# A recurrent block on one core: the third q/k unit and one constant row moved ahead of the second half's transposes, with other PSUM banks around them

## The chip, the core and the metric

The kernel runs on one NeuronCore of a Trainium2 chip. Its engines work side by side and meet only at semaphores: TensorE (PE; its weight loads are listed as PEld), VectorE (DVE), ScalarE (ACT), GpSimd (POOL), and SyncE (SP), which here only issues DMAs. Products land in PSUM, eight banks of 128 x 512 f32. The metric is the device time of one execution, in microseconds (us), as the median of three runs.

## What is computed

The input is (4, 1024, 128) in f32. Two layers, each `x + s(xn) * silu(f(xn))`, with xn the row-normalised x:

```python
# layer 0: attention in x with a bilinear score, times silu of a gated ternary MLP (512 hidden)
x = x + s * g
xn = _layernorm(x, axis=-1)
# layer 1, s: recurrence over 1024 steps, 8 heads of 64
q, k, v = xn @ Wq + bq, xn @ Wk + bk, xn @ Wv + bv
attn = softmax_over_heads(einsum('bhd,bhd->bh', q_t, k_t) * scale)
state = decay * state + (1 - decay) * attn[..., None] * v_t
out = layernorm((q * states + sigmoid(q * aug)) @ Wo + bo)
# layer 1, f: attention with 16 heads of 8 over 1024 tokens, plus top-2 of 8 experts
x = x + out * silu(attn_out + moe_out)
```

## The kernel before, in words

The four batch rows run one after the other (`for b in range(B)`), and each engine has its own program with an order written out by hand. Every value that needs more precision than one pass gives is carried as a high and a low part, so one product is three matmuls (`split3`). A "half" is 512 of the 1024 tokens.

Within a batch, layer 0 comes first, and ends with `residual(c)`, `block_stats(c)` and `block_normalise(c)` on DVE for each half c. POOL takes the inverse root of the variance between the last two (L866). PE then transposes the normalised half (`transposes`, L1110) into `T_BANKS[c]`, ACT copies the high part out (`split_head`, `xt_hi`, L944), DVE the rest (`split_rest`, `xt_lo`, L459).

Layer 1 is prepared by the part that the change touches, the bridge:

- `mq_units(c)` on PE: k and q of the 16-head attention for one half, four matmuls that need only the high part and two that need the low part, into `MQ_BANKS`. ACT adds the bias (`mq_head`, into `spl`, L999), DVE takes the low part (`mq_rest`, L548) and the largest absolute value (`mq_maximum`, L556).
- `qk_unit(u)` on PE: unit u of q and k of the recurrence, six matmuls of 512 columns into the two banks `QK_BANKS[u]`. ACT copies q (`q_unit`, into `qz`, L994), DVE multiplies by k (`product`, L541). Units 0 to 4 are in the bridge, 5 to 7 beside the attention. Units 0 to 3 read the first half only, so unit 2 needs neither the second half's transposes nor its split.
- `values_unit(0)` on PE and `values_in(0)` on DVE (L569, L574): the values of the first three token tiles.
- a bound of the scores: `bnd_in` after the four maxima, a product with ones on PE, a few small operations on DVE (from L611), `bnd_ok`.
- `stack(i)` on PE and `stacked(i)` on ACT (L1008, L1010), i = 0 to 3: the rows of the first group of four heads, with q and k for both halves. `stack(i)` needs `mq_rest(i)`.
- constant rows: ACT fills `k_st[:, g4, :]` for the groups 1 to 3 (three copies of 128 x 1024, L1027), POOL fills those of q after `bnd_ok` (L873).
- SP copies q and k of the groups 1 to 3 from `spl` to `k_st` and `q_st` in 72 small DMAs (L351). It starts when the three constant rows are filled and `mq_head(3)` is done.

The attention follows: 64 steps (`m_scores`, `m_values`), each with four score matmuls, four value matmuls and two exponentials on ACT (L1046), and a list `SIDE` of other pieces between them. Step 0 waits for `stacked(1)` and for `product(3)`, its order also puts it behind `stack(3)`, and it waits for a flag that DVE reads after `product(4)`. Step 16, the first of the second group of heads, waits until that group's DMAs have landed; these are among the first 64 of the 72.

PE's order in the bridge is: `mq_units(0)`, `g_transposes(1)`, `qk_unit(0)`, `qk_unit(1)`, `transposes(xnv, 6, 1)`, `values_unit(0)`, `mq_units(1)`, `qk_unit(2)`, `stack(0)`, the bound's product, `qk_unit(3)`, `stack(1)`, `stack(2)`, `qk_unit(4)`, `stack(3)`, step 0.

Of the kernel before, what the change touches and what calls it, by code (L numbers as in the profile page):

```python
# [14 lines left out]
ACT = mybir.ActivationFunctionType  # L15
# [6 lines left out]
B, S, D = 4, 1024, 128  # L22
NT = S // P
CH = 512
# [5 lines left out]
HM, HDM = 16, 8  # L30
# [17 lines left out]
H_BANKS = ((0, 1, 2, 3), (4, 5, 6, 7))  # L48
W3_BANKS, GT_BANKS = (0, 4), (1, 7)
PV_BANKS = (4, 5, 4, 5, 4, 5, 2, 3)  # L50
T_BANKS = (5, 6)
QK_BANKS = ((2, 3), (4, 5), (2, 3), (4, 5), (0, 1), (6, 7), (6, 7))
MQ_BANKS = (0, 1)
STK_BANKS = (6, 7, 6, 6)
NAT_LAST_BANK = 0
HEAD_ROWS = (slice(64, 80), slice(96, 112))

SIDE = {0: ("qk", 5), 1: ("qk", 6), 2: ("mv", 1), 3: ("q", 7), 4: ("mv", 2), 5: ("k", 7), 6: ("hs", 0), 7: ("hs", 1),
# [60 lines left out]
def build_program(nc, x, fw, lw, aw, wo, cst, cols, rows, bexp, out):  # L119
    with ExitStack() as ctx:  # L120
# [141 lines left out]
        def col(name, k=0):  # L262
            return cols_sb[:, COL[name] + k:COL[name] + k + 1]

        def up(signal, ins, n=1):

            signal.given += n
            return ins.then_inc(signal.sem, n)
# [96 lines left out]
        def _(v):  # L365
# [71 lines left out]
            for b in range(B):  # L437
# [19 lines left out]
                def split_rest(lo, hi, bank, c, sig_mm, n_mm, sig_hi, sig_lo):  # L457
                    v.wait_ge(sig_hi.sem, sig_hi.at(b, n_mm))
                    up(sig_lo, v.tensor_tensor(lo[:, c * CH:(c + 1) * CH], ps[:, bank, :],  # L459
                                               hi[:, c * CH:(c + 1) * CH].bitcast(F32), ALU.subtract))  # L460
# [75 lines left out]
                def product(u, bank):  # L536

                    c, m = u // KM, u % KM
                    v.wait_ge(qk_mm.sem, qk_mm.at(b, 2 * u + 2))
                    v.wait_ge(q_copy.sem, q_copy.at(b, u + 1))  # L540
                    up(prod_ok, v.scalar_tensor_tensor(prods[u], ps[:, bank, :], col("bk", m),  # L541
                                                       qz[:, m, c * CH:(c + 1) * CH], ALU.add, ALU.mult))

                def mq_rest(i):

                    c, j = i // 2, 1 - i % 2
                    v.wait_ge(mq_hi.sem, mq_hi.at(b, i + 1))
                    up(mq_lo, v.scalar_tensor_tensor(spl[:, 2 * j + 1, c * CH:(c + 1) * CH], ps[:, MQ_BANKS[i % 2], :],  # L548
                                                     col(("mbq", "mbk")[j]), spl[:, 2 * j, c * CH:(c + 1) * CH].bitcast(F32),
                                                     ALU.add, ALU.subtract))  # L550

                def mq_maximum(i):

                    c, j = i // 2, 1 - i % 2
                    v.wait_ge(mq_hi.sem, mq_hi.at(b, i + 1))
                    step(v.tensor_reduce(qk_max[:, 2 * j + c:2 * j + c + 1], spl[:, 2 * j, c * CH:(c + 1) * CH].bitcast(F32),  # L556
                                         AX.X, ALU.max, apply_absolute_value=True))
# [5 lines left out]
                def values_in(i):  # L563

                    tl = slice(3 * i, min(3 * i + 3, NT))
                    n_ = tl.stop - tl.start
                    v.wait_ge(mv_mm.sem, mv_mm.at(b, i + 1))
                    src = ps[:, SIDE_BANK, 0:n_ * (D + E)].rearrange("p (t n) -> p t n", n=D + E)
                    step(v.tensor_tensor(  # L569
                        vaug4[:, tl, :, 0:HDM], src[:, :, 0:D].rearrange("p t (h n) -> p t h n", n=HDM),  # L570
                        rows_sb[:, 3 * D:4 * D].rearrange("p (h n) -> p h n", n=HDM).unsqueeze(1)
                        .broadcast_to([P, n_, HM, HDM]), ALU.add))
                    own()
                    up(mv_ok, v.tensor_tensor(glog3[:, tl, :], src[:, :, D:D + E],  # L574
                                              rows_sb[:, 4 * D:4 * D + E].unsqueeze(1).broadcast_to([P, n_, E]), ALU.add))
# [15 lines left out]
                mq_rest(1)  # L591
                product(0, QK_BANKS[0][1])
                product(1, QK_BANKS[1][1])
                mq_maximum(0)
                mq_maximum(1)
                split_rest(xt_lo, xt_hi, T_BANKS[1], 1, xT_mm, 2, x_hi, x_lo)
                values_in(0)
                mq_maximum(2)
                mq_maximum(3)
                own()  # L600
# [3 lines left out]
                own()  # L604
                up(bnd_in, v.tensor_scalar(sm[:, 7, 0:HM], cst_sb[:, CBM:CBM + HM], qk_max[:, 6:7], None, ALU.mult))
                mq_rest(2)
                product(2, QK_BANKS[2][1])

                v.wait_ge(bnd_mm.sem, bnd_mm.at(b, 1))
                bound = ps[:, SIDE_BANK, 0:HM]  # L610
                step(v.tensor_reduce(flags[:, 1:2], bound, AX.X, ALU.min))  # L611
                own()
                step(v.tensor_scalar(flags[:, 2:3], flags[:, 1:2], -SAFE * HDM ** 0.5, None, ALU.is_ge))
# [298 lines left out]
        def _(a):  # L912
# [28 lines left out]
            for b in range(B):  # L941
                def split_head(hi, bank, c, sig_mm, n_mm, sig_hi):
                    a.wait_ge(sig_mm.sem, sig_mm.at(b, n_mm))
                    up(sig_hi, a.activation(hi[:, c * CH:(c + 1) * CH], ps[:, bank, :], ACT.Copy))  # L944
# [43 lines left out]
                def q_unit(u, bank):  # L988
                    c, m = u // KM, u % KM
                    if u == 0:  # L990
                        a.wait_ge(fin_ok.sem, fin_ok.at(b, 0))
                        a.wait_ge(stored.sem, stored.at(b, 0))
                    a.wait_ge(qk_mm.sem, qk_mm.at(b, 2 * u + 1))
                    up(q_copy, a.activation(qz[:, m, c * CH:(c + 1) * CH], ps[:, bank, :], ACT.Identity, bias=col("bq", m)))  # L994

                def mq_head(i):
                    c, j = i // 2, 1 - i % 2
                    a.wait_ge(mq_mm.sem, mq_mm.at(b, i + 1))
                    up(mq_hi, a.activation(spl[:, 2 * j, c * CH:(c + 1) * CH], ps[:, MQ_BANKS[i % 2], :], ACT.Identity,  # L999
                                           bias=col(("mbq", "mbk")[j])))  # L1000

                def stacked(i):
# [19 lines left out]
                mq_head(1)  # L1022
                q_unit(0, QK_BANKS[0][0])
                q_unit(1, QK_BANKS[1][0])
                for g4 in range(1, NG):
                    a.wait_ge(w3_mm.sem, w3_mm.at(b, 2))
                    up(kfill_ok, a.activation(k_st[:, g4, :], col("row24").broadcast_to([P, S]), ACT.Copy))  # L1027
                split_head(xt_hi, T_BANKS[1], 1, xT_mm, 2, x_hi)
                mq_head(2)
                mq_head(3)  # L1030
                q_unit(2, QK_BANKS[2][0])
                stacked(0)
                a.activation(mrow2[:, 0:1], ones[:, 0:1], ACT.Exp)
                q_unit(3, QK_BANKS[3][0])
                stacked(1)
                stacked(2)
                q_unit(4, QK_BANKS[4][0])
                stacked(3)

                for k_ in range(CYCLES):  # L1040
# [47 lines left out]
        def _(t_):  # L1088
# [9 lines left out]
            def with_high(out_, l_hi, l_lo, r_hi_):  # L1098

                mm(out_, l_hi, r_hi_, True, False)  # L1100
                mm(out_, l_lo, r_hi_, False, False)
# [38 lines left out]
            for b in range(B):  # L1140
# [6 lines left out]
                def lwp(at, n=P):  # L1147
                    return lw_hi[:, at:at + n], lw_lo[:, at:at + n]
# [158 lines left out]
                def mq_units(c):  # L1307

                    t_.wait_ge(x_hi.sem, x_hi.at(b, 1 + c))
                    for i, j in enumerate((1, 0)):  # L1310
                        with_high(ps[:, MQ_BANKS[i], :], *lwp(LM + j * D), xT(c)[0])
                    t_.wait_ge(x_lo.sem, x_lo.at(b, 1 + c))
                    for i, j in enumerate((1, 0)):
                        up(mq_mm, mm(ps[:, MQ_BANKS[i], :], lwp(LM + j * D)[0], xT(c)[1], False, True))

                def qk_unit(u):

# [12 lines left out]
                def values_unit(i):  # L1330

                    for t in range(3 * i, min(3 * i + 3, NT)):
                        at = (t % 3) * (D + E)
                        ins = split3(ps[:, SIDE_BANK, at:at + D + E], *tok(t), *lwp(LM + 2 * D, D + E))
                    up(mv_mm, ins)

                t_.wait_ge(lw_ok, 1)
# [2 lines left out]
                t_.wait_ge(pv_norm.sem, pv_norm.at(b, NT))  # L1340
                qk_unit(0)
                qk_unit(1)
                t_.wait_ge(ln_ok.sem, ln_ok.at(b, 2))
                transposes(xnv, T_BANKS[1], 1)
                values_unit(0)
                t_.wait_ge(mq_lo.sem, mq_lo.at(b, 2))
                mq_units(1)
                t_.wait_ge(prod_ok.sem, prod_ok.at(b, 1))
                qk_unit(2)
                stack(0)  # L1350
                t_.wait_ge(bnd_in.sem, bnd_in.at(b, 1))
                t_.wait_ge(mv_ok.sem, mv_ok.at(b, 1))
                up(bnd_mm, mm(ps[:, SIDE_BANK, 0:HM], ones, sm[:, 7, 0:HM], True, True))
                t_.wait_ge(prod_ok.sem, prod_ok.at(b, 2))
                qk_unit(3)
                t_.wait_ge(bnd_ok.sem, bnd_ok.at(b, 1))
                stack(1)
                t_.wait_ge(stk_ok.sem, stk_ok.at(b, 1))
                stack(2)
                t_.wait_ge(mq_lo.sem, mq_lo.at(b, 4))  # L1360
                qk_unit(4)
                t_.wait_ge(stk_ok.sem, stk_ok.at(b, 3))
                stack(3)

# [270 lines left out]
```

## Time and profile before

| what | us |
|---|---|
| median of three runs | 1064.15 (1063.66 to 1066.93) |
| the profiled execution | 1064.29 |
| its span, first to last instruction | 1062.5 |
| PE busy | 980.8 (92%) |
| ACT busy | 757.9 (71%) |
| DVE busy | 568.7 (54%) |
| POOL busy | 203.9 (19%) |

The profiled execution's own time is 1.8 us more than its span. The chain that ended last lies 72% on PE, 9% on DVE and 6% on ACT, so PE's queue sets most of the time, but the share is a mean over stages: in the bridge the chain passes from engine to engine. A batch takes some 255 us, and its bridge some 20.

### The profile page before, as it was taken

The page shows a single profiled execution, that of the slowest core. Times are in us where ns is not written, and L with a number is a line of the kernel's source. Part 1 is how long each engine was busy: PE and PEld are TensorE (multiplying, and loading weights), DVE is VectorE, ACT ScalarE, POOL GpSimd, SP SyncE. Part 2 cuts the span into 40 slices and gives each one's busy share as a digit, 9 for nine tenths or more (in the row PEclk, how much of TensorE's full clock was granted, in tenths as well). Part 3 has the DMA queues.
Part 4 walks back from the last instruction along what each step waited for, and adds up shares of the span by engine and source line. Part 5 has one row for each costly group of instructions (what it writes and reads, how often), then busy time and mean ns, then how long its engine had stood idle before and what let it go on. Part 6 is the DMA issues. An engine that isn't in the chain of part 4 may idle for free.

```text
span 1062.5 us, 16258 instructions
## 1 busy us (share of the span) xinstructions
PE 980.8 (92%) x6122; PEld 548.3 (52%) x6122; DVE 568.7 (54%) x1377; ACT 757.9 (71%) x922; POOL 203.9 (19%) x144
## 2 busy tenths in 40 slices
PE   2699899999999989999989989999998998999995
PEld 1588743344378853334347875334436886333431
DVE  6845744554465663472654574456447357346352
ACT  5253589988853479997955357998894436999885
POOL 3200021322120020240230002043022001114123
PEclk9799999999999989999999998999999999999998
DMA  6000033000000013200000002300000000320000
GB/s 236 1 2 1 1 49 62 1 2 1 1 22 2 1 19 50 43 2 2 1 20 2 1 1 39 51 22 1 1 1 21 2 1 10 50 33 1 1 1 23
DMA packets 14428, 20.66 MB, mean 19 GB/s; under 512 B 2848, under 2 KB 11136, under 8 KB 14080
## 3 DMA queue, kind: packets, MB, share of 16 engines
q1 hardware_dynamic: 14336, 19.41, 8.5%
q8 instruction: 60, 0.98, 0.4%
q14 instruction: 32, 0.26, 0.1%
HBM read 7.85 MB, written 2.10 MB: 9 GB/s over the span
## 4 chain that ended last, share of the span: by engine, by line
PE 72%; DVE 9%; ACT 6%; issue 6%; SPq 4%; POOL 2%; DMA 1%; DVEq 0%; POOLq 0%; ACTq 0%
PE ps L1090 69%; SPq L351 4%; ACT big L1046 3%; PE ps L1489 1%; DVE st L275 1%; DVE mx L483 1%; POOL st L866 1%; DVE xn L451 1%; DVE wk L731 1%; DVE wk L541 1%; ACT xn L1018 1%; DVE flags L419 1%; DVE wk L476 1%; PE ps L1110 1%; DVE qk_max L556 0%
## 5 line engine op out<-in xcount | busy, mean ns | idle before, releaser
L1046 ACT ACTIVATE big<-ps 128x1024 f32<-128x1024 f32 x512 | 493.8, 1034 | 50.5 <-PE ps L1090 48.6
L1090 PE MATMUL ps<-big,vaug 128*32 128x512 f32 x2048 | 272.6, 604 | 3.7 <-DVE wk L731 2.5
L1090 PE MATMUL ps<-hid 32*128 32x512 f32 x1024 | 130.5, 493 | 3.5 <-ACT big L1046 1.9
L1090 PE MATMUL ps<-hid,fw_sb 128*128 128x512 f32 x416 | 100.6, 396 | 0.0
L866 POOL TENSOR_TENSOR st<-st 128x4 f32<-128x4 f32 x16 | 16.2, 1011 | 433.9 <-DVE st L530 325.8
L965 ACT ACTIVATE wk<-ps,cols_sb 128x512 f32<-128x512 f32 x64 | 40.5, 687 | 78.3 <-PE ps L1090 74.2
L1090 PEld LDWEIGHTS ps<-hid 32*128 32x128 f32 x1024 | 49.1, 181 | 77.1 <-issue 42.0
L1090 PEld LDWEIGHTS ps<-hid,fw_sb 128*128 128x128 f32 x416 | 77.8, 188 | 17.6
L879 POOL TENSOR_TENSOR qz<-qz,wk 128x512 f32<-128x512 f32 x32 | 41.2, 1287 | 232.6 <-DVE wk L701 232.6
L1090 PEld LDWEIGHTS ps<-big,vaug 128*32 128x32 f32 x2048 | 41.0, 108 | 69.7 <-issue 41.6
L719 DVE SCALAR_TENSOR_TENSOR big<-ps,sm,big 128x128 f32<-128x128 f32 x128 | 44.2, 346 | 46.6 <-PE ps L1090 35.9
L1090 PE MATMUL ps<-wk,big 128*128 128x129 f32 x512 | 61.3, 275 | 2.4 <-ACT big L976 2.0
L1090 PEld LDWEIGHTS ps<-wk,big 128*128 128x128 f32 x512 | 60.5, 191 | 5.8 <-issue 4.1
L958 ACT ACTIVATE wk<-ps,cols_sb 128x512 f32<-128x512 f32 x32 | 21.9, 688 | 52.6 <-PE ps L1090 52.6
L1090 PE MATMUL ps<-xt_hi,lw_hi 128*128 128x512 f32 x112 | 53.2, 475 | 5.9 <-DVE wk L541 5.7
L1090 PEld LDWEIGHTS ps<-lw_hi,xt_hi 128*128 128x128 f32 x96 | 18.9, 197 | 60.4 <-DVE wk L719 33.6
L976 ACT ACTIVATE big<-ps 128x512 f32<-128x512 f32 x64 | 36.6, 602 | 14.2 <-PE ps L1090 14.1
L1090 PEld LDWEIGHTS ps<-xt_hi,lw_hi 128*128 128x128 f32 x112 | 22.7, 203 | 46.1 <-issue 8.4
L1090 PE MATMUL ps<-xt_hi,lw_lo 128*128 128x512 f32 x112 | 46.3, 414 | 0.0
L1090 PE MATMUL ps<-xt_lo,lw_hi 128*128 128x512 f32 x112 | 45.4, 419 | 0.5 <-DVE xt_lo L459 0.4
L688 DVE TENSOR_SCALAR wk<-ps,decay 128x512 f32<-128x512 f32 x32 | 25.9, 809 | 37.0 <-PE ps L1090 36.5
L467 DVE TENSOR_TENSOR hid<-wk,hid 128x512 fp32r<-128x512 f32 x64 | 44.3, 693 | 2.2
(210 smaller groups left out, 1630.5 us busy)
## 6 DMA issues: line engine op xcount, KB each, us to landing
hid<-spl SPq DMA_DIRECT2D x288, 32.0 KB
xnext<-in_x SPq DMA_DIRECT2D x4, 512.0 KB, 3.9
out<-qz SPq DMA_DIRECT2D x8, 256.0 KB, 2.3
big<-in_fw SPq DMA_DIRECT2D x1, 1877.0 KB, 9.2
wk<-in_lw SPq DMA_DIRECT2D x1, 1476.0 KB, 14.3
big<-in_fw SPq DMA_DIRECT2D x1, 939.0 KB, 11.0
cst_sb<-in_cst SPq DMA_DIRECT2D x1, 440.0 KB, 4.5
xn<-in_aw SPq DMA_DIRECT2D x1, 320.0 KB, 5.2
```

What stands on the lines that cost most here:

```text
L275: step(v.bn_stats(bn[:, t, :], src[:, t, :]))
L351: up(stk_in[g4 - 1], sp.dma_start(dst[to:to + HDM, g4, :].bitcast(F32), spl[at:at + HDM, 2 * j + which, :].bitcast(F32)), 16)
L467: up(hid_lo, v.tensor_tensor(hidden(buf, 1, m), src, hidden(buf, 0, m).bitcast(F32), ALU.subtract))
L688: up(v_copy, v.tensor_scalar(v1[u % 4], ps[:, SIDE_BANK, :], decay[:, KM + m:KM + m + 1], decay[:, 2 * KM + m:2 * KM + m + 1], ALU.mult, A ...
L719: ins = v.scalar_tensor_tensor(acc, src, weight, acc, ALU.mult, ALU.add)
L866: up(rstd_ok, g_.tensor_tensor(rstd[:, tl], var[:, tl], half[:, tl], ALU.pow))
L879: up(qs_ok, g_.tensor_tensor(qz[:, m, sl], qz[:, m, sl], v1[u % 4], ALU.mult))
L958: up(l1_act, a.activation(act32[n_ % 3], ps[:, L1_BANKS[c][m % 2], :], ACT.Silu, scale=col("w1s", m)))
L965: up(h_act, a.activation(act32[n_ % 3], ps[:, banks[m], :], ACT.Gelu, scale=col(name, m)))
L976: up(sc_exp, a.activation(big[:, h, jt // 2, (jt % 2) * CH:(jt % 2 + 1) * CH], ps[:, SC_BANKS[n_ % 4], :], ACT.Exp))
L1046: up(ms_exp, a.activation(prob[:, at:at + 2 * CH].rearrange("p (h n) -> p h n", n=CH), ps[:, bank:bank + 2, :], ACT.Exp, scale=HDM ** -0.5))
L1090: return t_.matmul(out_, lhsT, rhs, start=start, stop=stop, **kw)
```

## The change

It changes the order in the bridge and the banks that the order needs; no instruction is added or removed. On PE `qk_unit(2)` goes ahead of the second half's `transposes`, `values_unit(0)` and `mq_units(1)`, into the banks 6 and 0 (it was 2 and 3); it waits for `mq_rest(0)`. `qk_unit(3)` goes ahead of `stack(0)`, and `qk_unit(4)` ahead of `stack(1)` and `stack(2)`. The transposes land in bank 7, `mq_units(1)` in the banks 1 and 2, `values_unit(0)` in 6, the bound in 7. On ACT one of the three constant rows and `q_unit(2)` come ahead of `split_head`, the other two rows behind it. On DVE `split_rest` comes ahead of the first two maxima, and `product(2)` ahead of the other two.

```diff
-T_BANKS = (5, 6)
-QK_BANKS = ((2, 3), (4, 5), (2, 3), (4, 5), (0, 1), (6, 7), (6, 7))
-MQ_BANKS = (0, 1)
+T_BANKS = (5, 7)
+QK_BANKS = ((2, 3), (4, 5), (6, 0), (4, 5), (0, 1), (6, 7), (6, 7))
+MQ_BANKS = (0, 1, 1, 2)
+VALUES_BANKS, BOUND_BANK = (6, 7, 7), 7
...
# DVE
                 product(1, QK_BANKS[1][1])
+                split_rest(xt_lo, xt_hi, T_BANKS[1], 1, xT_mm, 2, x_hi, x_lo)
                 mq_maximum(0)
                 mq_maximum(1)
-                split_rest(xt_lo, xt_hi, T_BANKS[1], 1, xT_mm, 2, x_hi, x_lo)
                 values_in(0)
+                product(2, QK_BANKS[2][1])
                 mq_maximum(2)
                 mq_maximum(3)
...
                 mq_rest(2)
-                product(2, QK_BANKS[2][1])
 
                 v.wait_ge(bnd_mm.sem, bnd_mm.at(b, 1))
...
# ACT
-                for g4 in range(1, NG):
+                def k_row(g4):
                     a.wait_ge(w3_mm.sem, w3_mm.at(b, 2))
                     up(kfill_ok, a.activation(k_st[:, g4, :], col("row24").broadcast_to([P, S]), ACT.Copy))
+
+                k_row(1)
+                q_unit(2, QK_BANKS[2][0])
                 split_head(xt_hi, T_BANKS[1], 1, xT_mm, 2, x_hi)
+                k_row(2)
+                k_row(3)
                 mq_head(2)
                 mq_head(3)
-                q_unit(2, QK_BANKS[2][0])
+                q_unit(3, QK_BANKS[3][0])
                 stacked(0)
                 a.activation(mrow2[:, 0:1], ones[:, 0:1], ACT.Exp)
-                q_unit(3, QK_BANKS[3][0])
+                q_unit(4, QK_BANKS[4][0])
                 stacked(1)
                 stacked(2)
-                q_unit(4, QK_BANKS[4][0])
                 stacked(3)
...
# PE
                 qk_unit(1)
+                t_.wait_ge(mq_lo.sem, mq_lo.at(b, 1))
+                qk_unit(2)
                 t_.wait_ge(ln_ok.sem, ln_ok.at(b, 2))
                 transposes(xnv, T_BANKS[1], 1)
+                t_.wait_ge(q_copy.sem, q_copy.at(b, 3))
                 values_unit(0)
                 t_.wait_ge(mq_lo.sem, mq_lo.at(b, 2))
+                t_.wait_ge(q_copy.sem, q_copy.at(b, 1))
                 mq_units(1)
-                t_.wait_ge(prod_ok.sem, prod_ok.at(b, 1))
-                qk_unit(2)
+                t_.wait_ge(prod_ok.sem, prod_ok.at(b, 2))
+                qk_unit(3)
+                t_.wait_ge(mv_ok.sem, mv_ok.at(b, 1))
                 stack(0)
                 t_.wait_ge(bnd_in.sem, bnd_in.at(b, 1))
-                t_.wait_ge(mv_ok.sem, mv_ok.at(b, 1))
-                up(bnd_mm, mm(ps[:, SIDE_BANK, 0:HM], ones, sm[:, 7, 0:HM], True, True))
-                t_.wait_ge(prod_ok.sem, prod_ok.at(b, 2))
-                qk_unit(3)
+                up(bnd_mm, mm(ps[:, BOUND_BANK, 0:HM], ones, sm[:, 7, 0:HM], True, True))
+                t_.wait_ge(prod_ok.sem, prod_ok.at(b, 3))
+                t_.wait_ge(mq_lo.sem, mq_lo.at(b, 3))
+                qk_unit(4)
                 t_.wait_ge(bnd_ok.sem, bnd_ok.at(b, 1))
                 stack(1)
                 t_.wait_ge(stk_ok.sem, stk_ok.at(b, 1))
                 stack(2)
-                t_.wait_ge(mq_lo.sem, mq_lo.at(b, 4))
-                qk_unit(4)
                 t_.wait_ge(stk_ok.sem, stk_ok.at(b, 3))
                 stack(3)
```

## Rows read from the trace of the kernel before

**Rows 1.** The chain that ended last, whole span: start us, us, what

```profile
123.65 1.02 POOL st L866
...
378.43 1.02 POOL st L866
...
633.50 1.02 POOL st L866
...
888.57 1.02 POOL st L866
```

**Rows 2.** The timeline of ACT: start us, us, engine, line, what, count, idle before

```profile
140.00 1.94 ACT L1046 ACTIVATE big<-ps 128x1024 f32<-128x1024 f32 x2 [0.55 <-PE ps L1090]
...
395.14 1.94 ACT L1046 ACTIVATE big<-ps 128x1024 f32<-128x1024 f32 x2 [0.29 <-PE ps L1090]
...
650.19 1.94 ACT L1046 ACTIVATE big<-ps 128x1024 f32<-128x1024 f32 x2 [0.27 <-PE ps L1090]
...
887.96 2.93 ACT L1027 ACTIVATE hid<-cols_sb 128x1024 fp32r<-128x1024 f32 x3
891.48 0.60 ACT L944 ACTIVATE xt_hi<-ps 128x512 fp32r<-128x512 f32 x1 [0.58 <-PE ps L1110]
895.38 1.27 ACT L999 ACTIVATE spl<-ps,cols_sb 128x512 fp32r<-128x512 f32 x2 [3.30 <-PE ps L1090]
...
903.70 0.69 ACT L1008 ACTIVATE hid<-ps,bias_q 128x512 fp32r<-128x512 f32 x1 [0.67 <-PE ps L1090]
904.69 1.94 ACT L1046 ACTIVATE big<-ps 128x1024 f32<-128x1024 f32 x2 [0.30 <-PE ps L1090]
```

**Rows 3.** The timeline of SP's queue, fourth batch

```profile
896.73 48.84 SPq L351 DMA_DIRECT2D hid<-spl  x72
```

**Rows 4.** Windows of 1 us: window, sum, PE busy (count), granted clock, DMA share, GB/s

```profile
142.00:143.00 1.00, 0.01 (x2) 1.00 0.24 41
...
636.00:637.00 1.00, 1.00 (x8) 0.50 0.00 0
...
642.00:643.00 1.00, 1.00 (x4) 0.58 0.00 0
...
892.00:893.00 1.00, 1.00 (x6) 0.50 0.00 0
...
895.00:896.00 1.00, 1.00 (x5) 0.79 0.00 0
```

**Rows 5.** The timeline of DVE, bridge of the fourth batch

```profile
888.41 0.74 DVE L548 SCALAR_TENSOR_TENSOR spl<-ps,cols_sb,spl 128x512 fp32r<-128x512 f32 x1
...
892.63 1.27 DVE L556 TENSOR_REDUCE qk_max<-spl 128x1 f32<-128x512 f32 x2
893.81 0.68 DVE L459 TENSOR_TENSOR xt_lo<-ps,xt_hi 128x512 fp32r<-128x512 f32 x1
...
894.99 0.18 DVE L574 TENSOR_TENSOR cst_sb<-ps,rows_sb 128x24 f32<-128x24 f32 x1
896.10 1.28 DVE L556 TENSOR_REDUCE qk_max<-spl 128x1 f32<-128x512 f32 x2 [0.93 <-ACT spl L999]
...
897.95 0.75 DVE L548 SCALAR_TENSOR_TENSOR spl<-ps,cols_sb,spl 128x512 fp32r<-128x512 f32 x1
```

**Rows 6.** The timeline of PE, fourth batch

```profile
890.78 0.66 PE L1110 MATMUL ps<-cst_sb,xn 128*128 128x128 f32 x4 [2.75 <-DVE xn L451]
...
895.50 0.40 PE L1090 MATMUL ps<-xt_hi,lw_hi 128*128 128x512 f32 x1
...
896.67 0.40 PE L1090 MATMUL ps<-xt_hi,lw_lo 128*128 128x512 f32 x1
...
902.93 0.73 PE L1090 MATMUL ps<-spl,sel_r 32*128 32x512 f32 x2
...
904.15 0.50 PE L1090 MATMUL ps<-hid 32*128 32x512 f32 x4 [0.17 <-DVEq L630]
...
941.95 0.51 PE L1090 MATMUL ps<-hid 32*128 32x512 f32 x4 [0.35 <-DMA hid<-spl]
```

More of the change, by code:

```diff
@@ L547, in mq_rest @@
                     v.wait_ge(mq_hi.sem, mq_hi.at(b, i + 1))
-                    up(mq_lo, v.scalar_tensor_tensor(spl[:, 2 * j + 1, c * CH:(c + 1) * CH], ps[:, MQ_BANKS[i % 2], :],
+                    up(mq_lo, v.scalar_tensor_tensor(spl[:, 2 * j + 1, c * CH:(c + 1) * CH], ps[:, MQ_BANKS[i], :],
                                                      col(("mbq", "mbk")[j]), spl[:, 2 * j, c * CH:(c + 1) * CH].bitcast(F32),
@@ L567, in values_in @@
                     v.wait_ge(mv_mm.sem, mv_mm.at(b, i + 1))
-                    src = ps[:, SIDE_BANK, 0:n_ * (D + E)].rearrange("p (t n) -> p t n", n=D + E)
+                    src = ps[:, VALUES_BANKS[i], 0:n_ * (D + E)].rearrange("p (t n) -> p t n", n=D + E)
                     step(v.tensor_tensor(
@@ L606, in _ @@
                 mq_rest(2)
-                product(2, QK_BANKS[2][1])
                 v.wait_ge(bnd_mm.sem, bnd_mm.at(b, 1))
-                bound = ps[:, SIDE_BANK, 0:HM]
+                bound = ps[:, BOUND_BANK, 0:HM]
                 step(v.tensor_reduce(flags[:, 1:2], bound, AX.X, ALU.min))
@@ L998, in mq_head @@
                     a.wait_ge(mq_mm.sem, mq_mm.at(b, i + 1))
-                    up(mq_hi, a.activation(spl[:, 2 * j, c * CH:(c + 1) * CH], ps[:, MQ_BANKS[i % 2], :], ACT.Identity,
+                    up(mq_hi, a.activation(spl[:, 2 * j, c * CH:(c + 1) * CH], ps[:, MQ_BANKS[i], :], ACT.Identity,
                                            bias=col(("mbq", "mbk")[j])))
@@ L1310, in mq_units @@
                     for i, j in enumerate((1, 0)):
-                        with_high(ps[:, MQ_BANKS[i], :], *lwp(LM + j * D), xT(c)[0])
+                        with_high(ps[:, MQ_BANKS[2 * c + i], :], *lwp(LM + j * D), xT(c)[0])
                     t_.wait_ge(x_lo.sem, x_lo.at(b, 1 + c))
                     for i, j in enumerate((1, 0)):
-                        up(mq_mm, mm(ps[:, MQ_BANKS[i], :], lwp(LM + j * D)[0], xT(c)[1], False, True))
+                        up(mq_mm, mm(ps[:, MQ_BANKS[2 * c + i], :], lwp(LM + j * D)[0], xT(c)[1], False, True))
                 def qk_unit(u):
@@ L1333, in values_unit @@
                         at = (t % 3) * (D + E)
-                        ins = split3(ps[:, SIDE_BANK, at:at + D + E], *tok(t), *lwp(LM + 2 * D, D + E))
+                        ins = split3(ps[:, VALUES_BANKS[i], at:at + D + E], *tok(t), *lwp(LM + 2 * D, D + E))
                     up(mv_mm, ins)
```

## The prediction

> **What bounds the kernel now.** Read the chain that ended last first, to find the stage. In each batch it passes POOL's inverse root for the second half; I take its start as the zero T of that batch: 123.65, 378.43, 633.50 and 888.57 [rows 1]. The reader is to see that four batches repeat with some 255 us between them, so whatever the bridge gains counts four times. Then read the timeline of ACT for the first pair of exponentials, which is where the attention starts: T + 16.35, 16.71, 16.69 and 16.12 [rows 1, 2]. From there on the attention's order is untouched, so the sum of these four, 65.87 us, is what the change can move.
>
> Third, PE's timeline of the bridge. PE stands idle for 2.75 us ahead of the transposes, waiting for the normalised half [rows 6]. The windows of the granted clock show what follows: 0.50, the 1.2 GHz level, from T + 2.5 to T + 9.4 in the third batch and from T + 3.4 to T + 6.8 in the fourth [rows 4]. An idle window in the first batch, after the attention's start, left the clock at 1.00 [rows 4]. But the batch with the shorter low stretch starts its attention only 0.57 us sooner than the other [rows 2], so the clock is not what bounds the bridge: the chain passes through DVE and ACT, which wait for each other there.
>
> Fourth, SP's queue: 72 DMAs from T + 8.16 on in the fourth batch [rows 3]. Step 16 of the attention starts 45.22 us after their first, at 941.95, and waited for them [rows 3, 6]. That is 37.26 us after the first exponentials [rows 2, 6]. So there is a second bound: the attention gains nothing from starting earlier unless SP starts earlier too.
>
> **The change part by part**, on the fourth batch's rows, with PE at the full clock.
>
> *Unit 2 into the hole.* `mq_rest(0)` ends at T + 0.58 [rows 5] and frees bank 0. Six matmuls at a distance of 0.234 us (895.50 to 896.67 over five) [rows 6] take 1.4 us, T + 0.6 to T + 2.0; the transposes start at T + 2.21 as before [rows 6], so unit 2 costs nothing there. If the hole were not there it would cost its 1.4 us. What is left of the idle time is 1.15 us ahead of it and little behind it. On ACT one constant row (2.93 / 3 = 0.98 us) [rows 2] and `q_unit(2)` (0.7) fit ahead of `xt_hi`, which starts at T + 2.91 and ends at T + 3.51 [rows 2]. The unit's wait has the transposes queued behind it on PE; it is over before the half is normalised.
>
> *The split ahead of the maxima.* DVE's queue reaches that point at T + 4.06 (892.63) [rows 5], after `xt_hi`. `split_rest` takes 0.68 and ends at T + 4.74, where it was T + 5.92: 1.18 sooner. PE's last two products of `mq_units(1)` follow at T + 4.8. The two constant rows that are moved behind `xt_hi` end at T + 3.51 + 1.96 = T + 5.47, some 0.2 after the first of these products, so that they cost ACT's heads 0.2. The heads, 1.27 for two [rows 2], end at T + 6.7 (before: 896.65, T + 8.08). SP's first DMA moves from T + 8.16 to some T + 6.8; all 72 are issued as before, and step 16 may start at T + 52.0.
>
> *Values.* The two maxima and `values_in(0)` only change places with the split: they end at 895.17, T + 6.6, as now [rows 5]. `product(2)`, some 0.7, comes ahead of the second maxima, which start at T + 7.3 instead of T + 7.53 (896.10). From there 1.85 us pass to `mq_rest(2)` (897.95) [rows 5], which now ends at T + 9.05 + 0.10 + 0.75 = T + 9.85 (the 0.10 taken for the small operations of the values). The bound itself ends behind it in DVE's queue, by T + 10.7, sooner than PE asks for it.
>
> *PE's second half.* Unit 3 runs from T + 5.3 to T + 6.7, `stack(0)` 0.73 from then on. Then PE has nothing until the bound's small product near T + 9.1, and unit 4 waits for `mq_rest(2)` at T + 9.85. This is a new pause: 2.4 us in which only that small product runs. Unit 4 ends at T + 11.3, `stack(1)` and `stack(2)` start at T + 11.4. `stacked(1)` follows 0.77 after its product (902.93 to 903.70) [rows 2, 6], T + 12.2, and the pair, taken as the pair of heads at 1.27, ends at T + 13.45. `stack(3)` waits for it. From there to the first exponentials 1.76 us pass now (902.93 to 904.69) [rows 2, 6], of which 0.17 is the wait for DVE's flag; `product(4)` is then done some 1 us sooner, so 1.6 to 1.76: T + 15.1 to T + 15.25. I take T + 15.2.
>
> Sum without a low clock: 65.87 - 4 x 15.2 = 5.1 us, that is 1.1 to 1.5 a batch and 0.9 in the fourth. POOL's fill of the q rows starts with the bound and moves with it; nothing waits for it before SP's later half. Step 16 by the DMAs at T + 52.0 lies 0.5 us before T + 15.2 + 37.26 = T + 52.5: the second bound is just out of the way.
>
> *The clock.* No row shows the new pause. The nearest on one side is the idle time after the attention's start, which left the clock at 1.00; on the other the 2.75 us, which brought it to 0.50 in each batch seen [rows 4, 6]. Pauses of 2.4 us lie nearer the second, and where the low stretch starts differs from batch to batch (T + 2.5 or T + 3.4). Its price: unit 4 takes 1.4 more at half the clock, the stacks behind it some 0.5, so 1.9 a batch; bounds are 0 (no fall), and 3.45, half of a stretch of 6.9 us as in the third batch, all of it full of work that PE must do. I take two batches of four: 3.8 us.
>
> The Trainium skill, in TensorE: Matmul & The Clock Gate, section "HAM oscillation — how this bites in real kernels", says that waits between bursts of matmuls send the clock to its lower level again and again. By that rule, the trace agrees for the 2.75 us ahead of the transposes, and the change would trade that fall for one right ahead of the attention; the sum would be by the rule 5.1 - 4 x 1.9, a loss of 2.5 us, and by the idle window of the first batch a gain of 5.1.
>
> **The rivals.**
>
> *No fall, or in one batch at most.* Gain 5.1 to 3.2: 1059.2 to 1061.1. For it: 1.4 us idle are harmless, and the bound's product breaks the pause. Against it: that product is hardly work. Chance 0.36.
>
> *Two to four short falls.* 1064.29 - 5.1 + 3.8 = 1063.0 for two, 1064.9 for three, 1066.8 for four. Chance 0.40, the likeliest.
>
> *The DMAs hold step 16.* If ACT's two constant rows or the heads came later than reckoned and SP started at T + 8.16 as now, step 16 would stand at T + 53.4 in each batch, and the earlier start would be given back there: about 1064. Against it: 1.3 us between T + 6.8 and T + 8.16. Chance 0.06.
>
> *Slower: a long fall after the pause in every batch.* PE would go at 1.2 GHz from about T + 10 to T + 17, through unit 4, the stacks, step 0 and unit 5. 4 x 3.45 - 5.1 = 8.7 lost, 1073.0. It decides from 2.1 us a batch on ((5.1 + 3.2) / 4). For it: the third batch's 6.9 us. Against it: the fourth batch's 3.4 us, and that PE is full of work in unit 4. Chance 0.15.
>
> *The change does nothing:* `qk_unit(2)` never filled anything that bound, and the other moves cancel. Against it: `split_rest` waits 1.2 us behind maxima that no one needs yet. 1064, chance 0.03.
>
> **How the numbers follow.** 0.3% is 3.2 us, about what a measurement of this kernel can tell from no change. The profiled execution (1064.29) stands 0.14 above the median, so 1063.0 becomes 1062.9. Range 1059.0 (no fall) to 1066.8 (four short falls); it leaves out the long falls. Faster by over 3.2 us: the first rival and little else, 0.37. Slower: the long falls and a few mixed cases, 0.16. Between: 0.47.
>
> **What the profile of the changed kernel would show.** PE's idle time ahead of the transposes in two pieces, neither over 1.3 us, and the granted clock at 1.00 there. `xt_lo` at T + 4.1 to 4.7; SP's first DMA near T + 6.8; no idle PE at step 16. PE idle from T + 7.5 to T + 9.85 but for the bound's product. The first exponentials at T + 15.2 where the clock stays, near T + 17 where it falls. I am wrong if the clock falls ahead of the transposes still, if SP's first DMA stays at T + 8, or if the fall comes in all batches or in none.

## The result and the profile after

| | before | changed |
|---|---|---|
| median of seven runs each, us | 1065.23 (1063.66 to 1066.93) | 1070.16 (1068.01 to 1071.0) |
| the profiled execution | 1064.29 | 1068.89 |
| its span | 1062.5 | 1067.1 |

The ratio is 1.0042, with a 95% interval of 1.003 to 1.0054: the change makes the kernel 0.4% slower. The prediction was 1062.9 us, faster than before, with a range of 1059.0 to 1066.8. All readings of a profile below are of one execution per kernel. The two of this table lie 0.94 us (before) and 1.27 us (changed) under the medians of their seven runs.

First the zeros of the four batches and the first pairs of exponentials of the changed kernel, which answer to [rows 1] and [rows 2]: the chain that ended last (start us, us, what), then ACT's timeline.

```profile
123.38 1.02 POOL st L867
...
380.32 1.02 POOL st L867
...
635.71 1.02 POOL st L867
...
891.76 1.02 POOL st L867
```

```profile
141.16 1.94 ACT L1051 ACTIVATE big<-ps 128x1024 f32<-128x1024 f32 x2 [0.55 <-PE ps L1095]
...
397.10 1.94 ACT L1051 ACTIVATE big<-ps 128x1024 f32<-128x1024 f32 x2 [0.52 <-PE ps L1095]
...
652.55 1.94 ACT L1051 ACTIVATE big<-ps 128x1024 f32<-128x1024 f32 x2 [0.33 <-PE ps L1095]
...
908.85 1.94 ACT L1051 ACTIVATE big<-ps 128x1024 f32<-128x1024 f32 x2 [0.55 <-PE ps L1095]
```

The attention starts at T + 17.78, 16.78, 16.84 and 17.09, a sum of 68.49 us where it was 65.87: 2.62 us of the 4.6 us by which the span grew. The rest of a batch, counted from the first exponentials to the next batch's T (or the end), was 238.43, 238.36, 238.38 and 157.81 us and is 239.16, 238.61, 239.21 and 158.25: another 2.25 us. The first T is 0.27 us sooner (123.38, and 123.65 in [rows 1]). That adds up: 2.62 + 2.25 - 0.27 = 4.60.

PE's timeline of the fourth batch's bridge, T = 891.76, answers to [rows 6]:

```profile
892.40 0.51 PE L1095 MATMUL ps<-xt_hi,lw_hi 128*128 128x512 f32 x1 [1.17 <-DVE spl L549]
...
893.98 0.66 PE L1115 MATMUL ps<-cst_sb,xn 128*128 128x128 f32 x4
...
898.62 0.73 PE L1095 MATMUL ps<-spl,sel_r 32*128 32x512 f32 x2
900.92 0.40 PE L1095 MATMUL ps<-sm,cst_sb 128*128 128x16 f32 x2 [1.58 <-DVE sm L607]
901.66 0.77 PE L1095 MATMUL ps<-xt_hi,lw_hi 128*128 128x512 f32 x1 [0.35 <-DVE spl L549]
902.23 0.63 PE L1095 MATMUL ps<-xt_lo,lw_hi 128*128 128x512 f32 x1
902.65 0.63 PE L1095 MATMUL ps<-xt_hi,lw_lo 128*128 128x512 f32 x1
...
904.50 1.47 PE L1095 MATMUL ps<-spl,sel_r 32*128 32x512 f32 x4
906.85 0.73 PE L1095 MATMUL ps<-spl,sel_r 32*128 32x512 f32 x2 [0.89 <-ACT hid L1011]
```

The reader sees the order work as it was meant to. The 2.75 us hole is 1.17 us now, unit 2 runs in it, and the transposes start at T + 2.22, as before. After `stack(0)` (T + 6.86) comes the new pause: 1.58 us to the bound's small product at T + 9.16, then 0.35 more to unit 4 at T + 9.90. In the kernel before the same product had waited 0.37 us:

```profile
898.10 0.40 PE L1090 MATMUL ps<-sm,cst_sb 128*128 128x16 f32 x2 [0.37 <-DVE sm L605]
```

Unit 4's products start 0.42 us apart, not 0.234. The windows of the granted clock say why (answers to [rows 4]):

```profile
893.00:894.00 1.00, 1.00 (x6) 1.00 0.00 0
898.00:899.00 1.00, 1.00 (x5) 1.00 0.00 0
900.00:901.00 1.00, 0.08 (x1) 1.00 0.24 37
901.00:902.00 1.00, 0.65 (x3) 0.81 0.39 57
902.00:903.00 1.00, 1.00 (x3) 0.50 0.25 41
904.00:905.00 1.00, 1.00 (x3) 0.50 0.23 37
907.00:908.00 1.00, 0.89 (x4) 1.00 0.41 61
908.00:909.00 1.00, 0.80 (x5) 0.72 0.26 49
909.00:910.00 1.00, 1.00 (x3) 0.50 0.21 37
911.00:912.00 1.00, 1.00 (x6) 0.57 0.28 45
```

In these rows stand the window, its length, PE's busy time with the number of its instructions, the granted clock, the DMA share and GB/s. The clock is at 1.00 in the window of the old hole, falls to the 1.2 GHz level at the end of the new pause, comes back at some T + 13.3, and falls again at T + 16.7, into the first steps of the attention. All four batches do the like: windows of 0.5 us put the first fall at T + 10.2, 9.3, 9.9 and 9.9; in the first batch it lasts 10.2 us, in the others 3.4 us and another 3.4 us from T + 16.1 to 16.7 on.

DVE and SP did what was reckoned; the timelines of the two in the fourth batch:

```profile
895.81 0.68 DVE L460 TENSOR_TENSOR xt_lo<-ps,xt_hi 128x512 fp32r<-128x512 f32 x1
...
900.78 0.74 DVE L549 SCALAR_TENSOR_TENSOR spl<-ps,cols_sb,spl 128x512 fp32r<-128x512 f32 x1
```

```profile
898.44 48.67 SPq L352 DMA_DIRECT2D hid<-spl  x72
```

`xt_lo` starts at T + 4.05, `mq_rest(2)` at T + 9.02, SP at T + 6.68 (before T + 8.16, [rows 3]).

### The profile page after: what moved, and what is told of

Its sections match the earlier page's. It is cut to its first block, busy times and chain, and to the rows that moved or that the text cites. A ratio compares the mean times of both kernels' runs of the same rounds, so it can differ in the third digit from the quotient of the medians.

```text
span 1067.1 us, 16262 instructions
## 1 busy us (share of the span) xinstructions
PE 985.8 (92%) x6122; PEld 549.5 (51%) x6122; DVE 567.7 (53%) x1377; ACT 757.4 (71%) x922; POOL 203.8 (19%) x144
## 4 chain that ended last, share of the span: by engine, by line
PE 75%; DVE 10%; issue 6%; ACT 5%; POOL 2%; DMA 0%; POOLq 0%; DVEq 0%; ACTq 0%
PE ps L1095 73%; ACT big L1051 3%; PE ps L1497 1%; DVE wk L542 1%; DVE qk_max L557 1%; ACT xn L1019 1%; DVE st L276 1%; DVE mx L484 1%; POOL st L867 1%; DVE xn L452 1%; DVE wk L732 1%; DVE flags L420 1%; DVE wk L477 1%; DVE spl L549 0%; PE ps L1490 0%
## 5 line engine op out<-in xcount | busy, mean ns | idle before, releaser
L542 DVE SCALAR_TENSOR_TENSOR wk<-ps,cols_sb,qz 128x512 f32<-128x512 f32 x32 | 23.6, 747 | 43.7 <-PE ps L1095 34.2
```

## The experiments

The clock theory: the order itself is no slower; the new pause lowers PE's clock, and that costs the time. The rival, the order theory: units 3 and 4 ahead of the stacks, and the new queues on ACT and DVE, cost by themselves, and the clock goes with it. "Extra products" below are matmuls of 128x512 on PE into a bank that nobody reads then; they leave every result as it is. The kernel before was run again beside each group, and each ratio below is to that: a median of 1067.28 us for e1 to e4, 1065.06 for e5 to e7, 1065.71 for e8 to e10. Its own runs spread over 9 to 14 us in each group, so ratios of different groups that lie 0.1% apart are not told apart.

### e1: the new pause filled

```diff
                 stack(0)
+                for _ in range(8):
+                    mm(ps[:, 3, :], lw_hi[:, 0:P], xT(0)[0], True, True)
                 t_.wait_ge(bnd_in.sem, bnd_in.at(b, 1))
```

> The changed kernel plus eight products of 128x512 into bank 3, which nobody reads, on PE between stack(0) and the bound's product (8 x 0.234 = 1.9 us of the pause of 2.3 us). They add work and change no result. Clock theory: the pause at T + 7 to T + 9.9 is what lowers the clock, so with it filled the granted clock stays at 1.00 through the bridge in all four batches, the first exponentials come at T + 15.1 to 15.4 instead of 16.8 to 17.8, and the time is about 7 to 9 us under the changed kernel, 1059 to 1062. Rival, order theory: units 3 and 4 ahead of the stacks and the new order on DVE and ACT cost by their queueing, the clock only goes with it: the first exponentials stay at T + 16.5 or later, and the time at 1068 or more.

Measured: 1065.56 us, ratio to the kernel before 0.9982 (0.9965 to 0.9998). The first exponentials come at T + 15.64, 15.59, 15.29 and 15.93, sum 62.45 where the changed kernel has 68.49. The fall at T + 10 is gone. But the time did not reach 1059 to 1062: in the fourth batch (T = 889.39) the windows show a fall behind the stacks, at T + 13.7.

```profile
899.00:900.00 1.00, 0.85 (x6) 1.00 0.23 37
900.00:901.00 1.00, 1.00 (x6) 1.00 0.40 61
902.00:903.00 1.00, 0.12 (x2) 1.00 0.41 61
903.00:904.00 1.00, 1.00 (x3) 0.54 0.23 37
```

PE waits there for the stacks that ACT copies out (0.88 us at T + 13.5). The order theory fails: with eight products more than the changed kernel, in the same order, the attention starts 1.5 us sooner a batch.

### e2: the old hole filled, in the kernel before

```diff
                 qk_unit(1)
+                for _ in range(10):
+                    mm(ps[:, 6, :], lw_hi[:, 0:P], xT(0)[0], True, True)
                 t_.wait_ge(ln_ok.sem, ln_ok.at(b, 2))
```

> The kernel before plus ten products of 128x512 into bank 6, which nobody reads, on PE ahead of the wait for the second half (2.3 us of its 2.75 us hole). No result changes. Clock theory: no low stretch in the bridge; what it gives is only what the low stretch cost there, some 0.3 to 0.6 us a batch, so 1063 to 1064.5 where the kernel before has 1065.2. Rival: filling a hole helps by itself as much here as in the changed kernel, 4 us or more.

Measured: 1064.62 us, 0.9972 (0.9955 to 0.9989). No batch falls. The first exponentials are at T + 16.05, 15.80, 15.80 and 15.78; the sum is 63.43, 2.4 us less than before. So the falls behind the old hole had cost the attention's start 0.6 us a batch, the upper end of what was expected, and the rival (4 us or more) fails. Part of the gain is lost elsewhere, see the last section.

### e3: needed work in the pause

Unit 4 gets the banks 0 and 3 and goes between `stack(0)` and the bound.

```diff
-QK_BANKS = ((2, 3), (4, 5), (6, 0), (4, 5), (0, 1), (6, 7), (6, 7))
+QK_BANKS = ((2, 3), (4, 5), (6, 0), (4, 5), (0, 3), (6, 7), (6, 7))
...
                 stack(0)
+                t_.wait_ge(prod_ok.sem, prod_ok.at(b, 3))
+                qk_unit(4)
                 t_.wait_ge(bnd_in.sem, bnd_in.at(b, 1))
                 up(bnd_mm, mm(ps[:, BOUND_BANK, 0:HM], ones, sm[:, 7, 0:HM], True, True))
-                t_.wait_ge(prod_ok.sem, prod_ok.at(b, 3))
-                t_.wait_ge(mq_lo.sem, mq_lo.at(b, 3))
-                qk_unit(4)
...
-                t_.wait_ge(prod_ok.sem, prod_ok.at(b, 4))
+                t_.wait_ge(prod_ok.sem, prod_ok.at(b, 5))
                 mm(ps[:, S_FIRST, 0:1], ones, ones[:, 0:1], True, True)
```

> The changed kernel with qk_unit(4) in the banks 0 and 3, which are free by then, and placed between stack(0) and the bound's product, so that the new pause is filled by work that is needed and stack(1) no longer stands behind unit 4. Clock theory: unit 4 runs from T + 7.4 to T + 8.9, the clock holds, stack(1) starts with the bound at T + 10.7 instead of T + 11.4, first exponentials at T + 14.5 to 15.0, 1057 to 1060. If the 1.2 us pause between the bound's product and stack(1), together with the thin work of the stacks, lowers the clock too, exponentials come at T + 15.5 to 16 and the time is 1061 to 1065. Order theory: much the same gain, because unit 4 no longer delays the stacks, but with the clock low all the same.

Measured: 1062.09 us, 0.9954 (0.9935 to 0.9973): faster than both kernels, with no extra work. First exponentials at T + 14.48, 14.77, 15.18 and 14.73. The clock still falls in all four batches, at T + 11.6 to 14.4, so e3 gains what both theories allowed and does not tell them apart, as e1 does. What is left between the bound and step 0 is thin, here in the fourth batch (T = 886.94).

```profile
896.10 0.40 PE L1095 MATMUL ps<-sm,cst_sb 128*128 128x16 f32 x2
897.56 1.20 PE L1095 MATMUL ps<-spl,sel_r 32*128 32x512 f32 x4 [1.07 <-DVE bias_q L620]
899.64 0.75 PE L1095 MATMUL ps<-spl,sel_r 32*128 32x512 f32 x2 [0.89 <-ACT hid L1011]
900.32 0.59 PE L1095 MATMUL ps<-cst_sb 128*128 128x1 f32 x2
```

### e4 and e8: units 3 and 4 back behind the bound, without and with filling

e4 puts `qk_unit(3)` behind the bound's product and `qk_unit(4)` behind `stack(2)`, as they were, and ACT's copies with them; unit 2 stays early.

```diff
                 mq_units(1)
-                t_.wait_ge(prod_ok.sem, prod_ok.at(b, 2))
-                qk_unit(3)
                 t_.wait_ge(mv_ok.sem, mv_ok.at(b, 1))
                 stack(0)
                 t_.wait_ge(bnd_in.sem, bnd_in.at(b, 1))
                 up(bnd_mm, mm(ps[:, BOUND_BANK, 0:HM], ones, sm[:, 7, 0:HM], True, True))
-                t_.wait_ge(prod_ok.sem, prod_ok.at(b, 3))
-                t_.wait_ge(mq_lo.sem, mq_lo.at(b, 3))
-                qk_unit(4)
+                t_.wait_ge(prod_ok.sem, prod_ok.at(b, 2))
+                qk_unit(3)
...
```

> The changed kernel with qk_unit(3) and qk_unit(4), and ACT's copies of them, back at their old places behind the bound's product and behind stack(2); unit 2 stays ahead of the transposes. Clock theory: PE now has nothing from the end of stack(0), T + 7.3, until the bound's product at T + 9.1, and little work before it, so the clock falls in every batch; 1067 to 1071. Order theory: with the stacks no longer behind unit 4 the loss is gone, 1062 to 1066.

Measured: 1073.07 us, 1.0063 (1.0039 to 1.0086), the slowest of all. PE idles 1.13 us ahead of `stack(0)` and 1.77 us ahead of the bound; every batch falls at T + 9.4 to 10.2, and the first exponentials are at T + 16.94 to 18.20. These are readings of the fastest of its six runs (1068.84 us); no profile shows where the others lose 4 us more. The falls are those of the clock theory, though the median is 2 us above its range; the order theory's 1062 to 1066 fails.

e8 is e4 with twelve extra products behind `stack(0)`.

> The kernel of e4 (units 3 and 4 back behind the bound) with twelve products of 128x512 that nobody reads, into bank 3, between stack(0) and the bound's product. No result changes. Clock theory: e4 was slow by its still longer pause; filled (12 x 0.234 = 2.8 us of some 3), the clock holds there and the first exponentials come at T + 15.3 to 16 instead of 16.9 to 18.2: 1061 to 1064 where e4 had 1073. Order theory: units 3 and 4 so late cost by themselves, 1067 or more.

Measured: 1068.87 us, 1.0026 (1.0011 to 1.0041). Three batches keep the clock and start at T + 16.36, 16.35 and 16.36; the first falls at T + 7.9 already and starts at T + 18.16. The start misses the clock theory's T + 15.3 to 16, and the time is one that the order theory allowed (1067 or more). But the extra products were too many: `stack(0)` waits for the values until T + 6.7, so the twelve run past the moment when the bound is ready. The fourth batch's DVE had it at 900.63, and PE came to it at 901.74:

```profile
898.18 0.73 PE L1095 MATMUL ps<-spl,sel_r 32*128 32x512 f32 x2 [1.13 <-DVE cst_sb L575]
898.84 3.06 PE L1095 MATMUL ps<-xt_hi,lw_hi 128*128 128x512 f32 x12
901.74 0.29 PE L1095 MATMUL ps<-sm,cst_sb 128*128 128x16 f32 x2
```

So e8 does not tell the two theories apart for this order; it says only that filling takes 0.6 us off e4's first exponentials in the fourth batch. Taking the 1.1 us off too would give T + 15.25, but no run had that.

### e5 and e6: the thin stretches filled too

e5 is e3 with four extra products between the bound's product and `stack(1)` and three behind `stack(2)`; e6 is e1 with three behind `stack(2)`. All that are new go into bank 4. e5's edit, beside the one of e3:

```diff
...
+                t_.wait_ge(q_copy.sem, q_copy.at(b, 4))
+                for _ in range(4):
+                    mm(ps[:, 4, :], lw_hi[:, 0:P], xT(0)[0], True, True)
                 t_.wait_ge(bnd_ok.sem, bnd_ok.at(b, 1))
                 stack(1)
                 t_.wait_ge(stk_ok.sem, stk_ok.at(b, 1))
                 stack(2)
+                for _ in range(3):
+                    mm(ps[:, 4, :], lw_hi[:, 0:P], xT(0)[0], True, True)
                 t_.wait_ge(stk_ok.sem, stk_ok.at(b, 3))
```

> Unit 4 in the banks 0 and 3 in the pause, as in e3, plus products of 128x512 that nobody reads in the thin stretch behind it: four between the bound's product and stack(1), three between stack(2) and the wait of stack(3), in bank 4. No result changes. Clock theory: the thin stretch from T + 9.5 to T + 13 is what lowered the clock at T + 11.6 to 14.4 in e3; filled, no batch falls in the bridge, first exponentials at T + 14.4 to 14.7 (sum 58 to 59 where e3 has 59.2), the rest of each batch back from some 239.3 to 238.4 us; 1056 to 1059. Rival: the attention's 0.6 to 1 us come from its start against the DMAs and not from the clock; then the rest of a batch stays at 239.3 and the time at 1061 or more.

> The changed kernel with the eight extra products of e1 in the new pause and three more, in bank 4, between stack(2) and the wait of stack(3). No result changes. It shows what the change's order gives if the clock holds. Clock theory: falls vanish or become fewer than in e1, first exponentials at T + 15.1 to 15.4, rest 238.4 in most batches, 1059 to 1062. If the clock still falls near T + 14, as e1 with 1065.

Measured: e5 1061.56 us (1056.44 to 1065.0), 0.9953 (0.9932 to 0.9973); e6 1062.48 us, 0.9963 (0.994 to 0.9986). In the profiled execution of e5 (1057.87 us) three batches hold the clock and start at T + 14.43 to 14.46, and the rest of them is 238.25, 238.18 and 157.74 us, back to the kernel before; the first falls at T + 14.4. That settles the second part of the loss: the attention's 0.25 to 0.83 us a batch come from the clock, and not from its start against the DMAs, which is earlier here than anywhere. But the median of e5 misses the 1056 to 1059 that were expected and is only the level of e3; its runs spread over 8.6 us, and their mean clock with them (0.997 at 1056.44, 0.981 at 1065.0). The time of e6 lies 0.5 us above its range; it is the changed order with the clock held: T + 15.28 and 15.29 in the last two batches, which do not fall. The two falls left come at T + 14.9 and 15.6.

### e7 and e9: one line of the change alone

e7 is the kernel before with `split_rest` ahead of the first two maxima, nothing else. e9 fills the old hole besides, as e2.

```diff
                 product(1, QK_BANKS[1][1])
+                split_rest(xt_lo, xt_hi, T_BANKS[1], 1, xT_mm, 2, x_hi, x_lo)
                 mq_maximum(0)
                 mq_maximum(1)
-                split_rest(xt_lo, xt_hi, T_BANKS[1], 1, xT_mm, 2, x_hi, x_lo)
```

> The kernel before with one line moved: split_rest of the second half ahead of the first two maxima on DVE. The low stretch ahead of it stays, since PE's hole stays. xt_lo comes up to 1.2 us sooner where the clock is high and less where PE at 1.2 GHz is late with the products before it; SP's first DMA from T + 8.2 to 8.8 to T + 7.5 to 8.3; the bound follows by 0.3 to 0.9. First exponentials 0.2 to 0.6 sooner a batch, no new pause, so no new fall: 1 to 2 us under the kernel before. Rival: with the maxima late, the DVE queue ends where it ended, and nothing changes.

> The kernel of e7 (kernel before, split_rest ahead of the two maxima) with ten products of 128x512 that nobody reads, into bank 6, in the hole ahead of the transposes. No result changes. If the gain of the split and the cost of the fall are two separate things, all four batches have their first exponentials near T + 15.1, as the batches of e7 without a fall have; sum 60.3 and 1059 to 1062. Rival: the same sum as e7 (61.8), the hole's fall costs nothing once the split is early.

Measured: e7 1062.75 us, 0.9978 (0.9961 to 0.9994); e9 1060.95 us (1060.15 to 1061.29), 0.994 (0.9919 to 0.9961), the lowest median, though its interval overlaps those of e3, e5 and e6. The profiled execution of e7 is the fastest of its twelve (1060.66). In it the hole of 2.75 us lowers the clock in two batches (first exponentials at T + 15.95 and 15.42) and not in the other two (T + 15.33 and 15.06), a sum of 61.75. e9 has no fall in a bridge and T + 15.34, 15.06, 15.06 and 15.06. The fourth batch of e9, T = 886.70:

```profile
893.54 0.73 PE L1090 MATMUL ps<-spl,sel_r 32*128 32x512 f32 x2
895.20 0.40 PE L1090 MATMUL ps<-sm,cst_sb 128*128 128x16 f32 x2 [0.93 <-DVE sm L605]
895.44 0.48 PE L1090 MATMUL ps<-xt_hi,lw_hi 128*128 128x512 f32 x1
```

The bound's product comes at T + 8.50 and the pause ahead of it is 0.93 us, 0.65 less than in the changed kernel, because DVE goes straight to the maxima where the change has `product(2)` first (0.66 us from its start to theirs, 898.28 to 898.94 on DVE). PE has as much to do ahead of `stack(0)` in both, unit 2 here and unit 3 there, and starts it at T + 6.84 and 6.86. Against e2, where the clock does not fall either, the sum is 2.92 us less: what `split_rest` gains alone, 0.7 us a batch.

### e10: the changed kernel again

> The changed kernel itself, on the same chip as e8 and e9, to have it beside them: 1068 to 1071, with a fall of the clock at T + 9 to T + 11 in each batch. If the falls depend on where the pause lies, other starts of the falls than 9.3 to 10.2 may show, and the first exponentials between T + 16.5 and T + 18.

Measured: 1070.23 us, 1.0028 (1.0011 to 1.0045) against 1065.71 on that chip. Falls at T + 10.5, 9.7, 10.1 and 10.3, two of them 10.2 us long (in the first execution it was one), first exponentials at T + 17.56, 16.74, 16.84 and 17.72, all as expected.

## Why the prediction was wrong

**What held.** Unit 2 fits into the hole and delays nothing. `split_rest` 1.2 us sooner, SP 1.5 us sooner (T + 6.68, said 6.8), the bound's product at T + 9.16 (said 9.1), unit 4 at T + 9.90 (said 9.85). (The sum 9.05 + 0.10 + 0.75 is 9.90; the prediction wrote 9.85.) The attention without a fall was put at T + 15.2; e6 has T + 15.28. The DMAs hold nothing back: no wait of PE for them is seen in the changed kernel. The new pause was named, with 2.4 us, and so was the fall behind it, with 1.9 us a batch to the first exponentials: 17.12 on average against 15.28 is 1.84.

**The step that failed** is "I take two batches of four: 3.8 us", under the clock. All four fell, in both profiled executions of the changed kernel, eight batches of eight, and e1 shows that it was the pause: filled, the fall at T + 10 is gone. That alone moves 1063.0 to 1066.8, from a gain to a loss of 2.5 us, a sum that the prediction also had. It had said itself that 2.4 us lie nearer to the hole of 2.75, which had lowered the clock each time, and still priced the pause by half; and its first rival trusted the one small product inside the pause, which did not keep the clock up.

**The term that was missing**, and without which even four falls stay inside the range: the likeliest case ended the price of a fall at the first exponentials, and put the attention behind them at nothing. The clock comes back in three of the four batches when it was said to, but it falls again around `stack(3)` and step 0, now inside the attention, where PE is the bound: 2.25 us in sum. 1066.8 and 2.25 come to 1069.05; the profiled execution took 1068.89, and the median lies 1.27 above that. The rival "a long fall in every batch" (1073.0) had part of this mechanism with too high a price: one batch of four, and two of four in e10, had the long fall.

**What was read wrongly ahead of it.** From the 0.57 us between two batches the prediction took that the clock does not bound the bridge. Both of these batches had a fall; e2, with none, starts the attention 2.4 us sooner in sum. So nearly half of the 5.1 us that were booked for the new order is what the old falls cost.

**Where the gain would have been.** The kernels with filling let the orders be compared with the clock at 1.00 (batches without a fall; fourth batch):

| order | kernel | bound's product | `stack(1)` | `stack(3)` | first exponentials |
|---|---|---|---|---|---|
| before | e2 | T + 9.22 | T + 11.34 | T + 14.06 | T + 15.78 |
| changed | e6 | T + 9.46 | T + 11.47 | T + 13.55 | T + 15.29 |
| before, `split_rest` early | e9 | T + 8.50 | T + 10.62 | T + 13.33 | T + 15.06 |
| changed, unit 4 in the pause | e5 | T + 9.16 | T + 10.62 | T + 12.71 | T + 14.45 |

The last column is from ACT's timelines of e2, e6, e9 and e5, with T = 888.01, 887.01, 886.70 and 883.91:

```profile
903.79 1.94 ACT L1046 ACTIVATE big<-ps 128x1024 f32<-128x1024 f32 x2 [0.26 <-PE ps L1090]
902.30 1.94 ACT L1051 ACTIVATE big<-ps 128x1024 f32<-128x1024 f32 x2 [0.29 <-PE ps L1095]
901.76 1.94 ACT L1046 ACTIVATE big<-ps 128x1024 f32<-128x1024 f32 x2 [0.28 <-PE ps L1090]
898.36 1.94 ACT L1051 ACTIVATE big<-ps 128x1024 f32<-128x1024 f32 x2 [0.29 <-PE ps L1095]
```

One line, `split_rest` ahead of the maxima, is worth more (0.7 us a batch) than the whole change with its clock held (0.5). The pause is made on DVE. The early split brings `stack(0)` 1.2 us forward and the bound's product only 0.7 (e9 against e2), and `product(2)` ahead of the second maxima keeps that product back by 0.66 us (T + 8.50 against 9.16). Behind it unit 3 can start at once in e9, and unit 4 waits 0.35 us for `mq_rest(2)` in the changed kernel. None of this delays `stack(1)`: DVE's last operation of the bound ends at T + 10.57 in e9 and in e5 alike. The place of unit 4 decides the rest. Ahead of `stack(1)` it delays that by 0.85 us (e6 against e5). Between `stack(2)` and `stack(3)`, as before, `stack(3)` comes 2.7 us after `stack(1)`; with unit 4 elsewhere it comes 2.1 us after. (The bound's product of e6 is 0.3 us late by its eight extra products; unit 4 starts at T + 9.90 all the same.) PE's stacks and DVE's last operation, first in e9, then in e5:

```profile
897.10 0.17 DVE L619 TENSOR_REDUCE bias_q<-bias_w 128x4 f32<-128x16 f32 x1
897.32 1.19 PE L1090 MATMUL ps<-spl,sel_r 32*128 32x512 f32 x4 [0.24 <-DVE bias_q L619]
900.03 0.72 PE L1090 MATMUL ps<-spl,sel_r 32*128 32x512 f32 x2
...
894.31 0.17 DVE L620 TENSOR_REDUCE bias_q<-bias_w 128x4 f32<-128x16 f32 x1
894.53 1.20 PE L1095 MATMUL ps<-spl,sel_r 32*128 32x512 f32 x4
896.62 0.73 PE L1095 MATMUL ps<-spl,sel_r 32*128 32x512 f32 x2
```

So the early unit 2 brings nothing as the change uses it, but it lets units 3 and 4 run ahead of the bound, and with unit 4 in the pause the attention starts 0.6 us sooner than in e9. What that order loses again is the clock in the thin stretch behind it (e3).

**What stays open.** Why an equal hole of 2.75 us lowers the clock in some batches and not in others was not tried apart. Of e4, whose median is 4 us above its profiled execution, only part of the loss is explained. No run had the order of e3 with the clock held and nothing added.

## What to carry to other kernels

Filling a hole on TensorE with work from further back moves the hole: PE's idle time ahead of the second half's transposes went from 2.75 to 1.17 us in the fourth batch, and that from there to step 0 from 0.8 to 3.1. Look at the waits that stand behind the work that was taken, and count a pause with one small product in it (here 1.58 + 0.35 us) as one pause. A pause just ahead of a stage that TensorE bounds was paid twice here, in the bridge (1.84 us a batch) and in that stage (2.25 us in sum). Try the one-line reordering on the engine that feeds the wait (here the split ahead of maxima nobody waits for) by itself before rearranging everything around it. When a hole is filled, look for the work that stands between two steps of the chain, here unit 4 between two stacks.

## What the runs showed of the hardware

- Products of 32 rows (the stacks) with waits between them did not hold the clock: it fell in or right behind them in all batches of e1 (T + 13.7 to 15.3) and e3 (T + 11.6 to 14.4), with no pause of more than 1.1 us there in e3's fourth batch. With three extra products behind `stack(2)` it still fell in two batches of e6 and one of e5.
- Six kernels with extra products (e1, e2, e5, e6, e8, e9) have a longer rest of the first batch, 239.4 to 240.2 us, also where its clock does not fall in that part; in e9 it is 239.93 against 238.43 before. A wait of PE that the profile puts on nothing stands in it in each of the six, near 320 to 326 us, 0.5 to 1.5 us long; the first batch of the kernels without extra products has none of over 0.4 us. In e9 it stands at the start of the second half's first MLP products:

```profile
320.68 2.02 PE L1090 MATMUL ps<-wk,big 128*128 128x129 f32 x16 [0.84 <-ACT big L976]
323.87 0.39 PE L1090 MATMUL ps<-xt_hi,fw_sb 128*128 128x512 f32 x1 [1.17 <-issue]
```

  The cause was not tried. If the wait comes with the added instructions, the times of the six are longer by 0.5 to 1.5 us than the order and the clock alone would make them.
